# A hybrid conv and attention block on one core: the image loop is rotated, so that one image's experts run between the next image's feed-forward and q, k, v

## The reference

```
x  = x + BRA(x)                     # 16 x 16 windows of 4 pixels; q, k, v by window; each window picks the
                                    # 4 windows with the best mean-q . mean-k; attention over those 16 pixels;
                                    # plus a 5 x 5 depthwise convolution of v ("lepe")
x  = x + fc2(relu(dw3x3(fc1(x))))   # 128 -> 512 -> 128 channels, depthwise 3 x 3 between
t  = tokens of x                    # 1024 tokens of 128
t  = t + softmax(mask * q k^T) v Wo # 4 heads of 32, on LayerNorm(t); mask falls with the distance
u  = LayerNorm(t)
t  = t + u + sum over the top 2 of 8 experts of weight * (gelu(u w1 + b1) w2 + b2)
```

## Time and profile before

| | |
|---|---|
| median of 3 runs | 2216.06 us (2210.93 to 2216.33) |
| the profiled execution | 2220.89 us, span from first to last instruction 2219.0 us |
| mean granted clock of TensorE | 0.852 of 2.4 GHz |
| busy: TensorE, VectorE, GpSimd, ScalarE | 1603.0, 1488.3, 1143.7, 928.6 us |
| HBM | 46.56 MB read, 12.58 MB written, 27 GB/s |
| one turn of the loop (6 turns, images 0 to 5) | 256 us |

### The profile page before, as it was taken

One profiled execution on the slowest core, in us unless ns is written; L12 is line 12 of the kernel. 1 busy time (PEld: TensorE's weight loads), 2 busy tenths in 40 slices (PEclk: granted clock), 3 DMA queues, 4 the chain that ended last, 5 costly groups with the idle time before them and its releaser, 6 DMA issues.

```text
span 2219.0 us, 39848 instructions
## 1 busy us (share of the span) xinstructions
PE 1603.0 (72%) x15168; PEld 1059.0 (48%) x15168; DVE 1488.3 (67%) x2572; ACT 928.6 (42%) x1273; POOL 1143.7 (52%) x582
## 2 busy tenths in 40 slices
PE   2004457886879767886878767897678868898897
PEld 1002235553556435553556545564456535564565
DVE  3794569757785668758686578857686577841554
ACT  0000127522674227631564216732375226642683
POOL 0994789145960689226880569406890459600000
PEclk9557769997899878998889979998799988888898
DMA  4201200030000200030000300021000300000000
GB/s 130 76 0 38 77 1 2 1 125 1 1 2 30 98 1 1 2 104 23 1 1 1 126 1 1 1 67 59 1 1 1 115 1 1 1 1 11 1 2 10
DMA packets 26168, 62.04 MB, mean 28 GB/s; under 512 B 4192, under 2 KB 13408, under 8 KB 25824
## 3 DMA queue, kind: packets, MB, share of 16 engines
q0 software_dynamic: 9216, 33.56, 4.4%
q1 hardware_dynamic: 16736, 25.60, 3.6%
HBM read 46.56 MB, written 12.58 MB: 27 GB/s over the span
## 4 chain that ended last, share of the span: by engine, by line
PE 29%; issue 25%; DVE 21%; POOL 10%; ACT 3%; DMA 2%; DVEq 1%; POOLq 0%; SPq 0%; ACTq 0%
POOL KV L1237 8%; PE psB L404 7%; PE psB L536 5%; DVE P L1048 5%; DVE Q L948 3%; PE psA L585 2%; POOL KVSEL L1224 2%; PE psB L520 2%; PE psB L554 2%; DVE STACKED L1095 2%; DVE PROD L941 2%; DMA window_table<-KV 2%; PE psB L501 2%; PE psB L513 1%; PE psB L517 1%
## 5 line engine op out<-in xcount | busy, mean ns | idle before, releaser
L1253 POOL TENSOR_TENSOR XLEPE<-XLEPE,KV 128x1024 f32<-128x1024 f32 x200 | 498.8, 2494 | 16.7
L1237 POOL TENSOR_TENSOR KV<-KVSEL,Q 128x1024 f32<-128x1024 f32 x112 | 306.9, 2763 | 154.9 <-DVE KVSEL L917 119.8
L536 PE MATMUL psB<-W,P 128*128 128x128 f32 x2048 | 308.0, 298 | 102.7 <-DVE NEGMAX L1048 95.8
L1048 DVE CUSTOM_DVE_ANT_0 P<-psB,W 128x1024 f32<-128x1024 f32 x256 | 312.0, 1219 | 74.4 <-PE psB L404 44.5
L729 ACT ACTIVATE P<-P,NEGMAX 128x1024 f32<-128x1024 f32 x256 | 293.0, 1144 | 114.6 <-DVE NEGMAX L1056 112.6
L1224 POOL DMA_INDIRECT KVSEL<-window_table,CHOSEN x64 | 60.8, 950 | 536.8 <-DMA window_table<-KV 491.2
L536 PEld LDWEIGHTS psB<-W,P 128*128 128x128 f32 x2048 | 250.4, 152 | 176.9 <-issue 128.8
L1250 POOL TENSOR_SCALAR KV<-V_PAD,W 128x1024 f32<-128x1024 f32 x200 | 273.8, 1369 | 72.3 <-POOL XLEPE L1253 39.8
L737 ACT ACTIVATE PT<-psB 128x1024 f32<-128x1024 f32 x256 | 260.3, 1017 | 56.0 <-PE psB L536 54.3
L404 PE MATMUL psB<-TN,W 128*128 128x512 f32 (+1 forms) x512 | 252.2, 627 | 12.2 <-DVEq L1098 9.5
L948 DVE TENSOR_REDUCE Q<-PROD 128x128 f32<-128x2048 f32 x64 | 240.5, 3757 | 0.3
(11 more groups left out here) (117 smaller groups left out, 2094.8 us busy)
## 6 DMA issues: line engine op xcount, KB each, us to landing
window_table<-KV SPq DMA_DIRECT2D x8, 1024.0 KB, 6.1
X<-x_by_window_dram SPq DMA_DIRECT2D x8, 512.0 KB, 5.3
XLEPE<-x_dram SPq DMA_DIRECT2D x8, 512.0 KB, 3.9
out_dram<-PT SPq DMA_DIRECT2D x8, 512.0 KB, 3.8
W<-packed_dram SPq DMA_DIRECT2D x1, 3714.5 KB, 11.5
KVSEL<-window_table,CHOSEN POOLq DMA_INDIRECT x64, 5.4
FC<-packed_dram SPq DMA_DIRECT2D x8, 64.0 KB, 2.3
PROD<-gains_dram SPq DMA_DIRECT2D x1, 256.0 KB, 12.3
```

The lines of the kernel that those rows point to most:

```text
L536: mm = pe.transpose(ps[:, t * 128:(t + 1) * 128], P[:, i % P_BUFFERS, t * 128:(t + 1) * 128], ident)
L1048: dve.tensor_tensor_reduce(P[:, b, :], ps[:], w("band", at, at + TOK), 1.0, -3.0e38, ALU.mult, ALU.max, NEGMAX[:, b, 0:1]).then_inc(free, 1)
L1237: pool.tensor_tensor(PRODUCTS[i % 2].rearrange("p (k c) -> p k c", c=C), KVSEL[:, t, keys, 0:C], Q[:, t, q, :].unsqueeze(1).broadcast_to([ ...
L1253: pool.tensor_tensor(acc, acc, product, ALU.add).then_inc(lepe_done, 1)
```

## The change

The loop is rotated. A turn now begins with the attention of image n (its first block of scores has been taken out in the turn before) and ends with a stage called mixing. In mixing TensorE issues, for image n, the second LayerNorm and router; then for image n+1 `fc1` and `dw`, with `hidden 0`, `start`, `combine`, `hidden 1` of image n between them; then the eight experts of image n, and between them `fc2`, the first LayerNorm, v, q, k and the first scores of image n+1. The window projections of image n+2 go into the second LayerNorm, and 26 of the 36 window steps of image n+2 go between the sums of the experts on VectorE, where before 6 of them were there and 20 stood before the residual of `fc2`. So most of an image's window attention is done one stage earlier. `fc1` and the residual of `fc2` read XLEPE itself, and the copy `to_stream` goes. XLEPE is therefore loaded anew only after the residual of `fc2`. The second LayerNorm has buffers of its own (`LATER_TN`), the experts' hidden values use P's second and third buffer. ScalarE loads 7 tables per turn and not 6. Ahead of the loop, `mixing(None, 0, 1)` does image 0's feed-forward and q, k, v with 26 window steps of image 1. The last two turns are written out without the parts that have no image. GpSimd's code is unchanged.

```diff
+def mixing_order():
+    order = [("var", 1, 0), ("wo", 1), ("rstd", 1, 0), ("centred", 1, 1), ("fc1", 0), ("var", 1, 1), ("fc1", 1),
+             ("rstd", 1, 1), "router", ("dw", 0, 0), ("dw", 0, 1), ("hidden", 0), ("fc1", 2), "start", "combine",
+             ("hidden", 1), ("fc1", 3), ("dw", 1, 0), ("dw", 1, 1)]
+    beside = {0: ["fc2"], 1: [("centred", 0, 0), ("centred", 0, 1)], 2: [("var", 0, 0), ("var", 0, 1)],
+              3: [("rstd", 0, 0), ("rstd", 0, 1)], 4: ["v", ("q", 0), ("k", 0)], 5: [("q", 1), ("k", 1)],
+              6: [("q", 2), ("k", 2), ("scores", 0)], 7: [("q", 3), ("k", 3)]}
+    for e in range(EXPERTS):
+        order.append(("expert", e))
+        if e + 2 < EXPERTS:
+            order.append(("hidden", e + 2))
+        order += beside[e]
+    return order
 def main_order():
-    order = [("dw", 0, 0), ("dw", 0, 1), ("fc1", 2), ("fc1", 3), ("dw", 1, 0), ("dw", 1, 1)]
-    order += ["fc2", ("centred", 0, 0), ("centred", 0, 1), ("var", 0, 0), ("var", 0, 1),
-              ("rstd", 0, 0), ("rstd", 0, 1), "v"]
-    for h in range(HEADS_C):
-        order.append(("q", h))
-        if h == 3:
-            order.append(("turned", 0))
-        order.append(("k", h))
-        if 0 < h:
-            order.append(("scores", h - 1))
+    order = [("scores", u) for u in range(1, AHEAD)] + [("turned", 0)]
     for u in range(UNITS):
         if u > 0:
             order.append(("turned", u))
         if u + AHEAD < UNITS:
             order.append(("scores", u + AHEAD))
         order += {PROJECTED: [("wo", 0)], PROJECTED + 3: [("centred", 1, 0)]}.get(u, [])
-    order += [("var", 1, 0), ("wo", 1), ("centred", 1, 1), ("rstd", 1, 0), ("var", 1, 1), ("rstd", 1, 1),
-              "router", ("hidden", 0), "start", "combine", ("hidden", 1)]
-    for e in range(EXPERTS):
-        order.append(("expert", e))
-        if e + 2 < EXPERTS:
-            order.append(("hidden", e + 2))
-        if e in (NEXT_IMAGE, NEXT_IMAGE + 1):
-            order.append(("fc1", e - NEXT_IMAGE))
-    return order
+    return order + mixing_order()
...
+RING_B = EarlyRing(ORDER_B, [name for name in ORDER_B if is_next_image(name)], 3)
+PROJECTIONS_AFTER = {("centred", 1, 1): [(0, 0), (0, 1)], ("fc1", 0): [(0, 2), (0, 3)], ("var", 1, 1): [(1, 0), (1, 1)],
+                     ("fc1", 1): [(1, 2)], ("rstd", 1, 1): [(1, 3)]}
...
-EARLY_STEPS = 6
-MLP_STEPS = 20
+EARLY_STEPS = 26
+EARLY_LINKS = 11
...
+        HG = P[:, 1:3]
+        LATER_TN = [w("fc2"), PT[:, TURNED_BUFFERS - 1].rearrange("p t q -> p (t q)")[:, 0:HALF]]
...
-                    sp.wait_ge(x1_ready, m)
+                    sp.wait_ge(x2_ready, 2 * (2 * m - 1))
...
                 if first is not None:
-                    load_raster(first)
                     store_table(first)
-                store_out(n)
                 if after is not None:
                     x_is_free(after)
                     load_x(after)
+                if first is not None:
+                    load_raster(first)
+                store_out(n)
...
-                    mm = two_halves(ps, w("fc1", 128 * i, 128 * i + 128), XR, **whole)
+                    mm = two_halves(ps, w("fc1", 128 * i, 128 * i + 128), XLEPE, **whole)
...
+                    if name == ("hidden", 1):
+                        start_completed(n)
                     if second is not None and name in (("var", 1, 0), ("wo", 1)):
                         a_attended(second, int(name[0] == "wo"))
                     if first is not None:
+                        if name == ("wo", 1):
+                            a_windows(first)
+                        if name == ("centred", 1, 1):
+                            a_logits(first)
                         for t, p in PROJECTIONS_AFTER.get(name, []):
                             a_project(first, t, p)
-                        if name == ("centred", 1, 1):
-                            a_windows(first)
-                        if name == ("var", 1, 1):
-                            a_logits(first)
-                        if name == ("hidden", 3):
+                        if name == "router":
                             for h in range(2):
                                 a_values(first, h)
...
+            def mixing(n, second, first):
+                if n is not None:
+                    load_table(ACT.Sqrt, 0, n)
+                    deviation(1, 0, n)
                 if first is not None:
                     a_windows(first)
-                centred(1, 1, n)
-                deviation(1, 1, n)
-                load_table(ACT.Exp, 3, n)
-                act.wait_ge(rsub_ready, n + 1)
-                act.activation(PROBS, PROBS, ACT.Exp).then_inc(rexp_ready, 1)
-                load_table(ACT.Gelu, 4, n)
-                def gelu(e):
-                    evacuate(("hidden", e), n, hg_ready, lambda ps: act.activation(
-                        HG[:, e % 2, :], ps[:], ACT.Gelu, bias=col("b1", e)))
-                gelu(0)
-                evacuate("combine", n, combt_ready, lambda ps: act.activation(COMB_T[:], ps[0:EXPERTS, :], ACT.Copy))
-                gelu(1)
-                evacuate("start", n, acc_ready, lambda ps: act.activation(
-                    ACC.rearrange("p t c -> p (t c)"), ps[:], ACT.Copy))
-                for e in range(2, EXPERTS):
-                    gelu(e)
-                    if first is not None and e == 3:
-                        a_values(first)
-                    if second is not None and e - 2 in (NEXT_IMAGE, NEXT_IMAGE + 1):
-                        fc1(e - 2 - NEXT_IMAGE, second)
-                load_table(ACT.Exp, 5, n)
+                if n is not None:
+                    centred(1, 1, n)
+                if second is not None:
+                    fc1(0, second)
+                if n is not None:
+                    deviation(1, 1, n)
+                if second is not None:
+                    fc1(1, second)
+                if n is not None:
+                    load_table(ACT.Exp, 1, n)
+                    act.wait_ge(rsub_ready, n + 1)
+                    act.activation(PROBS, PROBS, ACT.Exp).then_inc(rexp_ready, 1)
+                if first is not None:
+                    a_values(first)
+                if second is not None:
+                    dw(0, 0, second)
+                    dw(0, 1, second)
+                if n is not None:
+                    load_table(ACT.Gelu, 2, n)
+                    gelu(0, n)
+                if second is not None:
+                    fc1(2, second)
+                if n is not None:
+                    evacuate("combine", n, combt_ready, lambda ps: act.activation(COMB_T[:], ps[0:EXPERTS, :], ACT.Copy))
+                    gelu(1, n)
+                    evacuate("start", n, acc_ready, lambda ps: act.activation(
+                        ACC.rearrange("p t c -> p (t c)"), ps[:], ACT.Copy))
+                if second is not None:
+                    fc1(3, second)
+                    dw(1, 0, second)
+                    dw(1, 1, second)
+                if n is not None:
+                    gelu(2, n)
+                    gelu(3, n)
+                if second is not None:
+                    for half in range(2):
+                        centred(0, half, second)
+                if n is not None:
+                    gelu(4, n)
+                if second is not None:
+                    load_table(ACT.Sqrt, 0 if n is None else 3, n)
+                    for half in range(2):
+                        deviation(0, half, second)
+                    load_table(ACT.Exp, 1 if n is None else 4, n)
+                if first is not None:
+                    a_exp(0, first)
+                if n is not None:
+                    if second is not None:
+                        load_table(ACT.Gelu, 5, n)
+                    gelu(5, n)
+                    gelu(6, n)
+                if second is not None:
+                    high(0, second)
+                if n is not None:
+                    gelu(7, n)
+                if second is not None:
+                    if n is not None:
+                        load_table(ACT.Exp, 6, n)
+                    for h in range(1, HEADS_C):
+                        high(h, second)
...
+            def fc2_residual(n, chain):
+                ps, free = arrived("fc2", n)
+                for half in range(2):
+                    chain.link(dve.scalar_tensor_tensor(out=XR[:, columns(half)], in0=ps[:, columns(half)], scalar=col("b_fc2"),
+                                                        in1=XLEPE[:, columns(half)], op0=ALU.add, op1=ALU.add))
+                    dve.sem_inc(x2_ready, 1)
+                dve.sem_inc(free, 1)
...
+            def mixing(n, second, first, chain):
+                front, steps = [], []
+                if first is not None:
+                    front = first_half(first)[1:]
+                    steps = second_half(first)[:EARLY_STEPS]
+                if n is not None:
+                    spread(1, 0, n)
```

(67 more changed lines are left out.)

348 lines of the change are left out of this document (150 added, 198 removed).

## The result

The changed kernel takes 2261.78 us (median of 4 runs, 2252.12 to 2267.86) against 2216.19 before (4 runs, 2210.93 to 2216.63): ratio 1.0207, 95% interval 1.0168 to 1.0247. Forecast were 2212 us and a range of 2172 to 2252. The profiled execution took 2260.87 us, its span 2259.3, which is 40.3 more than the span before.

The account below looks back on a forecast made before the run. Bound by hand-overs between engines, none of them full. Six turns +20, taps +5, start -6 and last turn -23 sum to -4 us, from the median of 2216.06 to 2212 us; range 2172 to 2252.

Parts of the forecast that it names:

- Step 1: Turn up to accumulate 0: TensorE's added `fc1` and `dw` bring expert 0 to VectorE at 996, against 964.4 before.
- Step 2: Accumulate 0 to scores u = 3: VectorE sets the pace, 102.3 us including waits, leaving each turn 3.3 us slower.
- the seam: Ring's wrap before scores 1, whose slot k 3 leaves last: TensorE starts it only after VectorE's last `low`, 1.0 us.
- Clock: TensorE pauses double the matmuls behind them; by that rule alone, second-half waits cost some +8 us per turn.
- Step 3: Attention: GpSimd's taps now cover all of it and slow VectorE's multiplies, 0.7 us in each of seven, 5 us.
- Step 4: Before the loop, image 0's new order reaches u = 3 at 326 to 328 instead of 333.2, gain 6 us.
- Step 5: Last turn, images 6 and 7, no window steps left: real overlap, 112 us instead of 135.1, gain 23.
- D: Taps bind: the next turn waits for GpSimd's taps, 4 us in six turns, 2236 us; chance 0.10.
- B: Slower: TensorE cold in the whole second half, VectorE meets it late at each expert, +32, 2248 us; chance 0.25.
- A: Level: the summed steps as forecast, 2212 us, own range 2196 to 2226; chance 0.43.

Follow-up runs that it names:

- e1: Changed kernel with the 8 sums of key products of window tile 0 ahead of accumulate 0 in VectorE's queue: 2222.81 us, ratio 1.0052.
- e4: e1 with the 8 sums of tile 1 also moved, ahead of the softmax of tile 0, on VectorE: 2185.41 us, ratio 0.9867.
- t1: Changed kernel with 13 instead of 25 taps of the depthwise 5x5 filter on GpSimd: 2209.69 us, ratio 0.9974.
- e5: e4 with VectorE subtracting the maximum of tile 0 before it waits for `fc2`: 2159.51 us, ratio 0.9747.
- f1: Changed kernel with 10 extra matmuls that nobody reads on TensorE behind k 3 of each image: 2267.07 us, ratio 1.0246.
- e6: e5 with q 3 and k 3 ahead of expert 7 on TensorE and low 3 ahead of accumulate 7 on VectorE: 2144.30 us, ratio 0.9678.
- e8: e6 with GpSimd issuing both tiles' gathers together and every engine's image loop written out: 2122.83 us, ratio 0.9581.
- f3: e8 with extra unread matmuls on TensorE behind expert 7, k 0, k 1 and scores 0: 2129.16 us, ratio 0.9636.

## Why the prediction was wrong

**What bounds the kernel, and the mechanism:** right. The 31 us idle of VectorE under experts, `dw` and `fc1`, called the weak point, is there (36.0 us), GpSimd stops after two products for 21.0 us, and e1 and e4 show that this is where the gain of the overlap goes: with 8 and with 16 sums moved ahead, 39 and 76 us come back. Of these the turns and the start, where the sums stand, hold 30 and 48; the attentions hold 7 and 27, where e4's earlier taps are mixed in.

**Step 1, to the first expert: the step that failed.** Forecast was 996 with a floor of 994 and an end of 999; measured is 1020.72. The turn itself begins later here (`spread` at 952.25, and at 933.32 in the kernel before), so on the scale of the forecast that is 1001.8. The instructions and their order were as walked; their clock was not. I took `dw` "nearer its 9.85", and without saying so I left the second LayerNorm at the length it has in the kernel before, though `fc1` now stands between its parts. In four of the six turns accumulate 0 comes 68.4 to 68.5 us behind `spread`, in one 65.2, and in the turn of image 4, where both stretches ran at 0.93 and 1.00 and not 0.87 and 0.88, 63.2, which would be 996.5. TensorE in these two turns (timeline), second `dw` pair:

```profile
1007.20 11.51 PE L505 MATMUL psB<-H_PAD,DIAG 32*32 32x512 f32 x288 [1.70 <-ACTq L687]
...
1538.26 9.74 PE L505 MATMUL psB<-H_PAD,DIAG 32*32 32x512 f32 x288 [1.70 <-ACTq L687]
```

That is 1.8 us of the 5.3 between the turns; 1.7 are in the first stretch and the rest on `fc1 3` (3.78 against 1.98). In that turn the whole stretch to u = 3 is 3.7 us longer than before, against a forecast of 3.3. So the term was mis-sized: its usual value was 5.8 us above mine, and the end of 999 was too near, because I charged a low clock to `dw` alone and not to the matmuls between waits ahead of it. t1 agrees: its first stretch is at full clock, and accumulate 0 comes 64.8 to 64.9 us behind `spread` in all six turns. The six turns are 24 of the 44 us missed, and nearly all of that is this step. What makes image 4's turn run at full clock I can't say.

**Step 2, accumulate 0 to u = 3:** right, 102.25 us against 102.3. The waits were 4.06 for `fc2` (3.9 to 5.6 forecast), 5.37 for expert 4 (3.6 to 5.4, and its cause as put, by e5), and 3.45 at the seam, where 1.0 was forecast. VectorE was busy 81.6 us in it (81 forecast). To the tenth it is luck: the waits for GpSimd's products (1.5 to 3 forecast) did not come, and the seam took their place, with the loop's jump, of which the forecast had nothing. And this part of VectorE's own time was taken as fixed; e4 shows that 16 sums of it were movable.

**Clock:** the rule of the Trainium skill on pauses (TensorE: Matmul & The Clock Gate, "Why this matters for your kernels") agrees with the trace in kind: 0.77 in the stretch with TensorE's long waits. I was wrong to look for its price in step 2, where it changed nothing; it fell on step 1, where VectorE waits for TensorE.

**Step 3, attention:** 5 forecast, 17.9 measured (21.8 from u = 3 to u = 31). VectorE's own busy time in the seven attentions rises by 3.8 us, near the forecast, but not where it was put. The multiplies are no dearer than before (mean of the 32 on tile 1's values, 3.09 us after and 3.22 before). It is the last window step, Q times SUMS, that has come under the taps: 0.69 us in every attention before, 0.69 to 2.32 after. The same attention, kernel before and changed kernel:

```profile
1174.74 0.69 DVE L954 TENSOR_TENSOR Q<-Q,SUMS 128x512 f32<-128x512 f32 x1
...
1204.17 1.81 DVE L989 TENSOR_TENSOR Q<-Q,SUMS 128x512 f32<-128x512 f32 x1
```

The other 18 of the 21.8 us are VectorE waiting, and of them the forecast had nothing. TensorE is busy 20.9 us more in the seven attentions for the same matmuls, at a granted clock of 0.88 to 0.90 against 0.90 to 0.95, and the first 15 us of a middle attention stand at 0.77 against 0.93 to 0.95. e1 has taps beside nearly all of attention, and its middle attentions but one have the old length (83.1 to 83.6 us); that one takes 86.6 us at the same clock of 0.91, with VectorE busy 76.6 us and not 73.6. In the middle turns u = 3 to u = 31 is 2.3 us longer and the tail behind it 1.3 shorter, so 1.0 is left; images 0, 1 and 6, whose attention before was 3 to 4 us shorter than the others', lost that advantage (2.6, 3.9, 5.3). Why TensorE is slower there is open. e1 speaks against the taps alone. It also speaks against the pause ahead of attention alone, since in its middle turns the clock is 0.50 in the 14 us ahead of u = 3 and 0.80 to 0.91 in the 15 us behind it (0.63 and 0.77 in the changed kernel). f1 tested the pause in one turn only. In e5 attentions of one program alternate between 78 us at a clock of 0.94 and 83 to 84 at 0.86 to 0.88; which of the two makes the other no run shows.

**Step 4, start:** gain 3.0, not 6. **Step 5, last turn:** gain 20.2, not 23; accumulate 0 after 53.2 us and not 50, u = 3 61.8 behind it (62 forecast).

**Rivals:** D did not happen, the last tap ends at 950.8 and its reader comes at 954.4, 3.6 us of margin (3.5 forecast). B had the order of size, +44 in six turns, +18, -3, -20 against its +48, +9, -5, -20, and still fell 14 us short. But it had the wrong place: it put the cold clock behind the first expert, where the time came out as in A, and the loss lies ahead of it. That B's number is the nearest is luck. I gave the warm clock the better chance on rows in which TensorE had just run dense work.

## What to carry to other kernels

When an order is rotated so that one stage covers another, list for each engine what stands behind the first wait of the new stage: an engine idle in front of an accumulate while its inputs for other work lie ready is a queue fault, and moving eight short steps ahead of it gave 39 us, at least 30 of them in the stretches concerned, where moving the matmul that it waits for gave minus 21. A stretch in which TensorE works between waits is to be priced at the clock that such a stretch has in the trace, not at the one of dense stretches. With sums early, maximum early, the seam closed and the loops written out the rotation is worth 4.2% and not minus 2.1%, though 1 to 1.2% of it is the loops alone.

## What the runs showed of the hardware

- A loop on the engines costs time, and not in its jump alone: 22 to 26 us in six turns for both kernels. Blocks of scores back to back start 1.53 us apart in the loop and 1.43 in the turns written out, within one program too. (The waits of the looped form are on values that depend on the loop's count; that this is the cause isn't shown.) The 2.4 us ahead of scores 1 in e6 are gone in e8.
- TensorE's granted clock differs between turns of one program that are the same in every instruction: 0.87 and 0.88 in one, 0.93 and 1.00 in another, 5.3 us apart.
- What GpSimd's taps cost VectorE depends on how the two happen to meet. A multiply of 128x2048 takes 2.29 us with GpSimd idle and from 2.28 to 4.47 beside it. The attention of image 3 takes 83.7 us in the kernel before with the four multiplies at 3.26 on the mean, 77.3 with 12 taps fewer (2.29), and 77.5 with all the taps and the loops written out (2.47).
- Matmuls that nobody reads, put into TensorE's pauses, raised its mean clock (0.876 to 0.899 from e8 to f3) and gained nothing in the time (2122.83 and 2129.16 us). In f1 the clock behind the filled pause rose in one middle turn of five.
